# Reordering four engines around the second layer's convolution and cross-attention in a two-layer decoder kernel

## The chip, the cores and the metric

One core of a Trainium2 chip runs the whole program in one launch. The metric is the device time of one execution in microseconds (us), as the median of several executions. PE is the tensor engine, DVE the vector engine, ACT the scalar engine, POOL the GpSimd engine, SP the queue that issues most transfers.

## The reference

Two decoder layers over x, 2 x 1024 tokens of 256 numbers, with a context of 77 rows per batch. Every sublayer is followed by a residual and a layer norm without scale.

```
x = ln(x + L0_attn(x))              # quaternion attention, 16 heads
x = ln(x + L0_xattn(ctx, x))        # two hops of attention to the 77 context rows
x = ln(x + L0_ffn(x))               # 8 experts, 256 tokens each, 256 -> 1024 -> 256, gelu
x = ln(x + L1_attn(x))              # see below
x = ln(x + L1_xattn(x, ctx, ctx))   # 16 heads of 16 numbers, 77 keys
x = ln(x + L1_ffn(x))               # quantised, 256 -> 768 -> 256

def L1_attn(x):                     # a causal convolution with a kernel of powers
    A = sigmoid(A_param)            # K[d, t] = C[d] * A[d]**t * B[d]
    out = conv(x, K) + D * x        # length 1024, per channel
    return layer_norm(x + gelu(out) @ W_proj.T + b_proj) * gamma + beta
```

## The kernel before

It is a kernel without a scheduler: for each engine the instructions are written out by hand in the order in which the engine runs them, and engines wait for each other on counting semaphores. An engine never passes an instruction that waits. X, the 16 tiles of 128 tokens, stays in SBUF. A group is 4 tiles (512 tokens), an expert 2 tiles. PSUM has 8 banks.

**The tail of the first attention.** Sixteen units (a pair of heads of one batch each) run PE, ACT (`exps`) and DVE; after them the second batch's output is turned (`out_turn`, L1721), divided by its denominators on DVE (L1134, L1136), turned again (`att_turn`, L1729), copied by ACT (L638), projected (`out_proj`, L1740), and added to X with a layer norm. A layer norm is always three steps: DVE makes the statistics (L1014, L1017), POOL the power -0.5 (`ln_power`, L388 and L390), DVE subtracts and multiplies (L1022). `ctxR`, the context repeated for each head, is copied by POOL (L466) and is wanted much later, by `context_values`.

**The experts.** For expert e PE runs `hidden(e)` (L1897), ACT the gelu (L701), PE `output(e)` (L1910) into bank 4 or 5, then DVE `expert_stats(e)` (L1281, L1014, L1017) and `expert_norm(e)` (L1022). Before that sum POOL has added the bias b2 to the expert's two tiles of X (L491, one instruction per expert). PE's order is hidden(0), hidden(1), output(0), output(1), hidden(2), hidden(3), and then `x_group_turn` (L1759), which transposes group 0 for the convolution and waits for the norms of experts 0 and 1, output(2), output(3), `projected(0)` and so on. Between the first of these PE makes the keys and values of the second cross-attention (`context_values`, L1885), which DVE masks (L1241, L1243). After the last of them DVE makes the powers of A (L1252) and the convolution's kernels (L1256).

**The convolution** of a group is `convolved(g, k, part)` on DVE (L1269 and L1270, a scan; L1274 and L1275), `conv_gelu` on ACT (L706), `projected(g)` on PE (L1924), then on DVE `conv_out` (L1294), `conv_stats`, `conv_affine(g, 0)` (L1311), `conv_affine(g, 1)` (L1313), `x_stats`, `x_norm`. POOL makes the two operands `XB3[g]` = X + b_proj (L495) and `XG[g]` = X + beta (L498).

**The second cross-attention** starts before the last expert and the last group's convolution are done. It has 32 steps n (a tile and one of two halves of the heads). Each is: `xa_scores(n)` on PE (L1983), `lowest(n)` on DVE (L1351), `numer(n)`, eight exponentials on ACT (L743), `denom(n)` on DVE (L1358, L1359), `weights(n)` on POOL (L524), `p_turn(n)` on PE (L1996) and `p_evac(n)` on ACT (L753, L754). PE's loop at step n issues xa_scores(n + 3) ahead of p_turn(n). Other work is tied to numbers of the loop: `x_turn4` and `queries(1)` to n = 3 and 4 on PE, the four parts of the last group's convolution to n = 0 to 3 on DVE, its gelu to n = 4 on ACT, `projected(3)` to n = 6 on PE. From n = 8 PE also makes the values of the group before (`xa_values`, L2014), the first of which waits for `conv_out(3)`. Everything behind that, to the end of the program, is the same in both kernels.

## Time and profile before

| | us |
|---|---|
| median of 3 runs | 819.36 (818.97 to 822.05) |
| the profiled execution, its time | 822.18 |
| its span, first to last instruction | 820.5 |
| PE busy / DVE / ACT / POOL | 720.7 / 529.3 / 552.2 / 197.8 |

The profiled execution took 1.7 us more than its span, and 2.8 us more than the median of the other runs.

A timeline row gives start, duration, engine, line, operation, tile shapes and count; in brackets stands the idle time just before it and what ended it. A row of the chain of waits gives start, duration and what ran; "issue" is time in which the engine waited for nothing that the profile shows. A row of stretches gives, after the length, the busy time of each engine, then the granted clock of PE (1.00 is 2.4 GHz, 0.50 is 1.2 GHz).

### The profile page before, as it was taken

To read this page: it belongs to the slowest core of one execution; us is meant where nothing else is said; L and a number is where in the kernel's file an instruction comes from. 1 tells how busy PE (TensorE), PEld (TensorE's weight loads), DVE (VectorE), ACT (ScalarE), POOL (GpSimd) and SP (SyncE) were. 2 spreads that over 40 slices of the span, in tenths; PEclk is the share of its full clock that TensorE was granted. 3 is DMA by queue.
4 is the path that set the end of the run, shared out by engine and by line. 5 is a ranking of instruction groups with operands and counts; after the bars stand their busy time and mean duration, and the time that the engine had idled before them with its cause. 6 is when DMAs were issued, how large, how long until landed. Compare 5 with 4: busy or idle time off the path is not lost.

```text
span 820.5 us, 10712 instructions
## 1 busy us (share of the span) xinstructions
PE 720.7 (88%) x3774; PEld 394.6 (48%) x3774; DVE 529.3 (65%) x1215; ACT 552.2 (67%) x971; POOL 197.8 (24%) x232
## 2 busy tenths in 40 slices
PE   4999999899999998999959999678898999992496
PEld 2652222112222227888858887444454744440385
DVE  4694646925223217495458659868976687988886
ACT  3659999999999991653122343586786533798991
POOL 1561142201010003021373113454553200000012
PEclk9899999999999999999989999869998999997698
DMA  7312113122363240230606000002000000000002
GB/s 193 122 26 44 35 26 86 31 66 48 69 193 83 61 121 1 103 103 2 205 0 206 1 1 0 1 0 77 6 34 1 1 0 1 0 1 0 0 26 77
DMA packets 57373, 42.12 MB, mean 51 GB/s; under 512 B 36866, under 2 KB 54120, under 8 KB 57192
## 3 DMA queue, kind: packets, MB, share of 16 engines
q1 hardware_dynamic: 57176, 41.31, 18.1%
q8 instruction: 30, 0.49, 0.3%
q10 hardware_dynamic: 144, 0.13, 0.1%
q14 instruction: 23, 0.19, 0.1%
HBM read 28.59 MB, written 4.46 MB: 40 GB/s over the span
## 4 chain that ended last, share of the span: by engine, by line
PE 60%; ACT 19%; DVE 14%; issue 4%; SPq 1%; DMA 1%; POOL 1%; POOLq 0%; DVEq 0%; ACTq 0%
ACT arena L627 12%; PE banks L1599 8%; PE banks L2139 7%; PE banks L1897 7%; PE banks L1910 6%; PE banks L2147 5%; PE banks L1585 4%; PE banks L1569 3%; PE banks L1759 2%; PE banks L1924 2%; PE banks L1983 2%; DVE arena L1429 2%; PE banks L2027 2%; ACT arena L830 1%; PE banks L1996 1%
## 5 line engine op out<-in xcount | busy, mean ns | idle before, releaser
L627 ACT ACTIVATE arena<-banks 128x1024 f32<-128x1024 f32 x256 | 239.9, 1045 | 8.3 <-PE banks L1599 6.1
L1599 PE MATMUL banks<-arena 128*32 128x512 f32 x1024 | 137.2, 608 | 4.2 <-DVE arena L1091 4.0
L1585 PE MATMUL banks<-arena 64*128 64x512 f16 x512 | 86.6, 385 | 9.0 <-ACT arena L627 5.8
L2139 PE MATMUL banks<-arena 128*128 128x512 f32 x192 | 83.1, 593 | 1.1 <-DVE arena L1445 0.9
L743 ACT ACTIVATE arena<-banks,arena 128x77 f32<-128x77 f32 x256 | 59.3, 366 | 24.5 <-DVE arena L1351 24.5
L388 POOL TENSOR_SCALAR arena<-arena 128x2 f32<-128x2 f32 (+1 forms) x38 | 11.0, 289 | 260.8 <-DVE arena L1017 260.8
L1585 PEld LDWEIGHTS banks<-arena 64*128 64x128 f16 x512 | 20.8, 93 | 108.3 <-ACT arena L627 96.8
L2147 PE MATMUL banks<-arena 128*128 128x256 f32 x192 | 44.4, 396 | 26.8 <-ACT arena L851 26.8
L701 ACT ACTIVATE arena<-banks,arena 128x256 f32<-128x256 f32 x64 | 26.9, 471 | 53.0 <-PE banks L1897 53.0
L1022 DVE TENSOR_SCALAR arena<-arena 128x256 f32<-128x256 f32 x96 | 45.2, 524 | 22.9 <-POOL arena L390 22.9
L2139 PEld LDWEIGHTS banks<-arena 128*128 128x128 f32 x192 | 36.2, 190 | 47.4 <-issue 43.4
L1910 PE MATMUL banks<-arena 128*128 128x256 f32 x256 | 57.0, 382 | 0.0
L1897 PE MATMUL banks<-arena 128*128 128x256 f32 x256 | 56.2, 379 | 0.0
L524 POOL TENSOR_TENSOR arena<-arena 128x616 f32<-128x616 f32 x32 | 40.8, 1275 | 58.7 <-DVE arena L1359 58.7
L2147 PEld LDWEIGHTS banks<-arena 128*128 128x128 f32 x192 | 38.3, 200 | 33.3 <-ACT arena L851 27.6
L1910 PEld LDWEIGHTS banks<-arena 128*128 128x128 f32 x256 | 48.9, 192 | 7.0 <-issue 0.4
L1897 PEld LDWEIGHTS banks<-arena 128*128 128x128 f32 x256 | 48.5, 190 | 6.5
L809 ACT ACTIVATE arena<-banks 128x512 f32<-128x512 f32 x48 | 28.2, 612 | 30.4 <-PE banks L2139 30.4
L1091 DVE COPY arena<-banks 128x512 f32<-128x512 f32 x16 | 10.9, 683 | 53.8 <-PE banks L1599 53.8
L1599 PEld LDWEIGHTS banks<-arena 128*32 128x32 f32 x1024 | 20.5, 108 | 44.9 <-issue 42.7
L1014 DVE BATCH_NORM_STATS2 arena<-arena 128x6 f32<-128x256 f32 x112 | 40.2, 414 | 1.1
L642 ACT ACTIVATE arena<-banks 128x1024 f32<-128x1024 f32 x20 | 20.6, 1028 | 29.1 <-PE banks L1759 28.3
(253 smaller groups left out, 1299.6 us busy)
## 6 DMA issues: line engine op xcount, KB each, us to landing
arena<-in_L_ffn_w SPq DMA_DIRECT2D x16, 1024.0 KB, 7.5
w_kept<-arena SPq DMA_DIRECT2D x3, 768.0 KB, 3.7
arena<-w_kept SPq DMA_DIRECT2D x3, 768.0 KB, 4.7
arena<-in_x SPq DMA_DIRECT2D x4, 512.0 KB, 8.4
out_x<-arena SPq DMA_DIRECT2D x3, 512.0 KB, 2.9
arena<-in_L_ffn_b SPq DMA_DIRECT2D x1, 1024.0 KB, 8.5
arena<-in_L_ffn_w_gate SPq DMA_DIRECT2D x1, 768.0 KB, 7.4
arena<-in_L_ffn_w_up SPq DMA_DIRECT2D x1, 768.0 KB, 9.2
```

The lines of the kernel that those rows point to most:

```text
L524: pool.tensor_tensor(Ex[n % 4], Ex[n % 4], rdx[:, n % 4, :, None].to_broadcast([P, HC, LC]), ALU.mult).then_inc(sem("xa_w"), 1)
L627: act.activation(PT[kt % 2][:, half], PS[:, 2 * (n % 3):2 * (n % 3) + 2, :], ACT.Exp, scale=DH ** -0.5 / QK_UP ** 2).then_inc(sem("exp_don ...
L743: ins = act.activation(Ex[n % 4][:, h, :], PS[:, 2 * (n % 2) + h // 4, LC * (h % 4):LC * (h % 4) + LC], ACT.Exp, scale=-1.0, bias=mxs[:, 8 ...
L809: act.activation((GF if n < IC * G4 else UF)[:, c, 512 * g:512 * g + 512], bank(2 + n % 4), ACT.Copy).then_inc(sem("gu"), 1)
L1014: ins = dve.bn_stats(bstat[:, at + j, :], view(j))
L1022: ins = dve.tensor_scalar(dst(j), src(j), mv[:, at + j, 0:1], rstd[:, at + j:at + j + 1], ALU.subtract, ALU.mult)
L1585: mm = pe.matmul(bank(2 * (n % 3) + h), KT[u % 2][64 * h:64 * h + 64, P * kt:P * kt + P], QT[u % 2][64 * h:64 * h + 64, 512 * half:512 * h ...
L1599: mm = pe.matmul(PS[32 * j:32 * j + 32, 6, :], VS[w][:, kt, h, :], PT[kt % 2][:, half, h, :], start=(kt == 0), stop=(kt == TB - 1))
L1897: mm = pe.matmul(PS[:, f // 2, 256 * (f % 2):256 * (f % 2) + 256], W1r[r][:, k, P * f:P * f + P], XT[:, k, TE * P * e:TE * P * e + TE * P] ...
L1910: mm = pe.matmul(bank(4 + e % 2)[:, D * j:D * j + D], hT[e % 2][:, f, P * j:P * j + P], W2r[r][:, f, :], start=(f == 0), stop=(f == FT - 1))
L2139: mm = pe.matmul(bank(2 + n % 4), (wgT if n < IC * G4 else wuT)[:, k, P * c:P * c + P], XT[:, k, 512 * g:512 * g + 512], start=(k == 0), s ...
L2147: mm = pe.matmul(PS[:, t % 8 // 2, D * (t % 2):D * (t % 2) + D], UF[:, c, P * t:P * t + P], wdT[:, c, :], start=(c == 0), stop=(c == IC - 1))
```

## The change

It edits the order of instructions, and with it some buffers:

1. After the attention units DVE runs `out_norm(3)` behind the divisions of steps 4 and 5 instead of ahead of them. The copy `ctxR` moves from POOL to ACT.
2. POOL adds b2 for experts 0 and 1, once the third set of context values is masked (l1_kv at 4, not 6), and spreads the other six: 2 behind the norm of expert 0, 4 behind that of expert 1. DVE makes the powers ahead of the last two sets of context values, and the norm of expert 0 ahead of the last one; the kernels follow the norm of expert 1.
3. POOL makes X + b_proj and X + beta apart, each earlier. For group 2 they use the buffers of group 0 (`XB3[2]` = `XB3[0]`).
4. PE runs `xa_scores(0)` and `xa_scores(1)` ahead of `projected(2)` (now in banks 5 and 7), then `xa_scores(2)`, the first tile of `output(7)` (now in bank 6), `p_turn(0)`, `xa_scores(3)`, the second tile of `output(7)`, then the loop from n = 1. The turn of group 3, which waits for the last expert's norm, stands behind `p_turn(2)` instead of ahead of the loop. DVE, ACT and POOL are put in a like order; the last convolution's parts stand at n = 2 (two), 3 and 4, its gelu at n = 5.

```diff
@@ pool
-                if q == 3:
-                    pool.wait_ge(sem("mem_ctxT"), 1)
-                    pool.wait_ge(sem("pv_done"), TB * UN)
-                    for b in range(B):
-                        pool.tensor_copy(ctxR[:, b], ...).then_inc(sem("ctx_rep"), 1)
...
-            pool.wait_ge(sem("l1_kv"), 6)
-            for e in range(E):
...
+            pool.wait_ge(sem("l1_kv"), 4)
+            x_plus_b2(0)
+            x_plus_b2(1)
...
             for e in range(E - 2):
                 ln_power(LN_CN[e], 2, 4)
                 g = e // 2
+                pool.wait_ge(sem("ln_c"), e + 1)
+                if e == 0:
+                    x_plus_b2(2)
+                    x_plus_b2(3)
                 if e == 1:
+                    for n in range(4, E):
+                        x_plus_b2(n)
                     pool.wait_ge(sem("l1_wT"), 4)
-                if e in (1, 3):
+                    x_plus_bproj(0)
+                    x_plus_beta(0)
+                if e in (3, 5):
+                    if e == 5:
+                        pool.wait_ge(sem("ln_d2"), 1)
                     x_plus_bproj(g)
-                    x_plus_beta(g)
-                if e in (3, 5):
                     ln_power(LN_DN[2 * g - 2], 4)
                     ln_power(LN_DN[2 * g - 1], 4)
+                    pool.wait_ge(sem("ln_d2"), g)
+                    x_plus_beta(g)
             ln_power(LN_CN[E - 2], 2, 4)
-            x_plus_bproj(2)
-            x_plus_beta(2)
-            ln_power(LN_DN[4], 4)
-            ln_power(LN_CN[E - 1], 2, 4)
+            pool.wait_ge(sem("ln_c"), E - 1)
             x_plus_bo(0)
             weights(0)
             weights(1)
+            ln_power(LN_DN[4], 4)
             for n in range(UX):
                 if n + 2 < UX:
                     weights(n + 2)
+                if n == 0:
+                    ln_power(LN_CN[E - 1], 2, 4)
@@ act
+            act.wait_ge(sem("pv_done"), TB * UN)
+            for b in range(B):
+                act.activation(ctxR[:, b], ..., ACT.Copy).then_inc(sem("ctx_rep"), 1)
...
-            xT_evac(CONV_N[3], 3, 4)
             for n in range(UX):
...
                 p_evac(n)
+                if n == 2:
+                    xT_evac(CONV_N[3], 3, 6)
...
-                if n == 4:
+                if n == 5:
                     conv_gelu(3, 0)
                     conv_gelu(3, 1)
@@ dve
-            out_norm(3)
             for q in range(4, 8 + 3):
...
+                if q == 5:
+                    out_norm(3)
...
+            value_rows(0, 4)
+            value_rows(1, 0)
+            value_rows(2, 1)
+            powers()
+            value_rows(3, 2)
+            expert_stats(0, 4)
+            expert_norm(0, 4)
+            value_rows(4, 3)
+            for e in range(1, E - 2):
                 expert_stats(e, 4)
                 expert_norm(e, 4)
                 g = e // 2
+                if e == 1:
+                    kernels()
...
-            conv_out(2)
-            conv_stats(2)
...
             lowest(0)
+            lowest(1)
+            denom(0)
+            conv_out(2)
+            lowest(2)
+            denom(1)
+            conv_stats(2)
             conv_affine(2, 0)
-            lowest(1)
+            lowest(3)
+            denom(2)
             conv_affine(2, 1)
             expert_stats(E - 1, 4)
-            lowest(2)
+            lowest(4)
             expert_norm(E - 1, 4)
-            denom(0)
-            denom(1)
-            between = {0: lambda: convolved(3, 0, 0), 1: lambda: convolved(3, 0, 1), 2: lambda: convolved(3, 1, 0), 3: lambda: convolved(3, 1, 1),
+            denom(3)
+            between = {2: lambda: (convolved(3, 0, 0), convolved(3, 0, 1)), 3: lambda: convolved(3, 1, 0), 4: lambda: convolved(3, 1, 1),
@@ pe
             output(6)
             queries(0)
-            projected(2)
             xa_scores(0)
             xa_scores(1)
-            output(7)
+            projected(2)
             xa_scores(2)
-            x_group_turn("ln_c", E, CONV_N[3], 3, b0=4)
-            for n in range(UX):
+            output(7, range(0, 1))
+            p_turn(0)
+            xa_scores(3)
+            output(7, range(1, TE))
+            for n in range(1, UX):
...
                 p_turn(n)
+                if n == 2:
+                    pe.wait_ge(sem("proj_y"), 3)
+                    x_group_turn("ln_c", E, CONV_N[3], 3, b0=6)
```

How the rows on an engine move, before first and then changed (line numbers are each kernel's own).

DVE, behind the last attention unit; L1091 is the last unit's copy, L1022 `out_norm(3)`, L1134 and L1136 the divisions of steps 4 and 5:

```order
L1091 COPY arena<-banks 128x512
L1022 TENSOR_SCALAR arena<-arena 128x256 x2
L1134 RECIPROCAL arena<-banks 128x32
L1136 TENSOR_TENSOR arena<-banks,arena 128x256 x2
L1134 RECIPROCAL arena<-banks 128x32
L1136 TENSOR_TENSOR arena<-banks,arena 128x256 x2
```

```order
L1107 COPY arena<-banks 128x512
L1149 RECIPROCAL arena<-banks 128x32
L1151 TENSOR_TENSOR arena<-banks,arena 128x256 x2
L1149 RECIPROCAL arena<-banks 128x32
L1151 TENSOR_TENSOR arena<-banks,arena 128x256 x2
L1038 TENSOR_SCALAR arena<-arena 128x256 x2
```

The norm stands behind both divisions.

POOL, at the start of the experts; L491 (now L487) is the sum with b2, L388 and L390 (now L392 and L394) a norm's power, L495 and L498 (now L496 and L499) the operands of group 0:

```order
L491 TENSOR_TENSOR arena<-arena 128x512 x8
L388 TENSOR_SCALAR arena<-arena 128x2
L390 TENSOR_TENSOR arena<-arena 128x2
L388 TENSOR_SCALAR arena<-arena 128x2
L390 TENSOR_TENSOR arena<-arena 128x2
L495 TENSOR_TENSOR arena<-arena 128x1024
```

```order
L487 TENSOR_TENSOR arena<-arena 128x512 x2
L392 TENSOR_SCALAR arena<-arena 128x2
L394 TENSOR_TENSOR arena<-arena 128x2
L487 TENSOR_TENSOR arena<-arena 128x512 x2
L392 TENSOR_SCALAR arena<-arena 128x2
L394 TENSOR_TENSOR arena<-arena 128x2
L487 TENSOR_TENSOR arena<-arena 128x512 x4
L496 TENSOR_TENSOR arena<-arena 128x1024
```

Two sums instead of eight stand ahead of the first norm's power, two more ahead of the second's, and four behind both.

PE, from `queries(0)` (L1968, now L2012) to the turn of group 3 (L1759, now L1800); L1924 (now L1968) is `projected(2)`, L1983 (now L2027) scores, L1910 (now L1954) `output(7)`, L1996 (now L2041) a `p_turn`:

```order
L1968 MATMUL banks<-arena 128x512 x4
L1924 MATMUL banks<-arena 128x256 x8
L1983 MATMUL banks<-arena 128x308 x4
L1910 MATMUL banks<-arena 128x256 x16
L1983 MATMUL banks<-arena 128x308 x2
L1759 MATMUL banks<-arena 128x128 x8
```

```order
L2012 MATMUL banks<-arena 128x512 x4
L2027 MATMUL banks<-arena 128x308 x4
L1968 MATMUL banks<-arena 128x256 x8
L2027 MATMUL banks<-arena 128x308 x2
L1954 MATMUL banks<-arena 128x256 x8
L2041 MATMUL banks<-arena 128x128 x4
L2041 MATMUL banks<-arena 104x128
L2027 MATMUL banks<-arena 128x308 x2
L1954 MATMUL banks<-arena 128x256 x8
L2027 MATMUL banks<-arena 128x308 x2
...
L1800 MATMUL banks<-arena 128x128 x8
```

Behind the last row but one stand the rest of steps 1 and 2 (three `p_turn` in all and the scores up to n = 5) before the turn of group 3.

## Rows read from the trace of the kernel before

**Rows 1.** The chain of waits, around the first turn for the convolution

```profile
401.72 13.81 PE banks L1897 x64
415.53 8.54 issue
424.08 1.94 PE banks L1759 x8
426.02 14.39 PE banks L1910 x64
```

**Rows 2.** POOL's timeline at the start of the experts

```profile
403.90 14.77 POOL L491 TENSOR_TENSOR arena<-arena 128x512 f32<-128x512 f32 x8 [32.13 <-issue]
...
422.19 0.22 POOL L388 TENSOR_SCALAR arena<-arena 128x2 f32<-128x2 f32 x1 [2.53 <-DVE arena L1017]
```

**Rows 3.** DVE's timeline, same stretch

```profile
385.94 0.49 DVE L1243 TENSOR_TENSOR arena<-arena 128x128 f32<-128x128 f32 x2
...
401.76 0.43 DVE L1241 TENSOR_TENSOR arena<-banks,arena 128x256 f32<-128x256 f32 x1 [6.69 <-PE banks L1885]
...
403.88 5.49 DVE L1252 TENSOR_TENSOR_SCAN arena<-arena 128x1023 f32<-128x1023 f32 x2
...
420.34 0.69 DVE L1281 TENSOR_TENSOR arena<-banks,arena 128x512 f32<-128x512 f32 x1
...
423.24 0.73 DVE L1022 TENSOR_SCALAR arena<-arena 128x256 f32<-128x256 f32 x2 [1.14 <-POOL arena L390]
```

**Rows 4.** PE's timeline behind the first attention's last unit

```profile
310.13 1.97 PE L1721 MATMUL banks<-arena 128*128 128x128 f32 x16 [1.44 <-DVE arena L1091]
```

**Rows 5.** The chain of waits, same stretch

```profile
310.64 2.50 DVE arena L1022 x2
...
314.25 0.99 PE banks L1729 x4
```

**Rows 6.** Stretches: length, busy PE, PEld, DVE, ACT, POOL, then PE's clock

```profile
312.00:314.20 2.20, 0.10 (x1) 0.00 (x0) 2.17 (x5) 0.00 (x0) 0.99 (x1) 1.00 0.00 0
314.20:318.00 3.80, 3.75 (x18) 3.73 (x19) 1.99 (x6) 0.76 (x2) 0.00 (x0) 0.55 0.00 0
```

**Rows 7.** The chain of waits, second cross-attention

```profile
503.12 3.69 PE banks L1924 x16
...
520.96 1.97 PE banks L1759 x8
...
544.38 1.15 ACT arena L706 x2
...
551.39 4.49 PE banks L1924 x16
```

**Rows 8.** Groups by line, 502 to 552 us: total, mean ns of one

```profile
L743 ACT ACTIVATE arena<-banks,arena 128x77 f32<-128x77 f32 x72 | 16.6, 353 | 15.0 <-DVE arena L1351 15.0
L524 POOL TENSOR_TENSOR arena<-arena 128x616 f32<-128x616 f32 x8 | 11.1, 1398 | 14.4 <-DVE arena L1359 14.4
...
L1022 DVE TENSOR_SCALAR arena<-arena 128x256 f32<-128x256 f32 x4 | 7.5, 1926 | 1.6 <-POOL arena L390 1.6
```

**Rows 9.** Groups by line, DVE, 521 to 545 us

```profile
L1358 DVE TENSOR_REDUCE arena<-arena 128x8 f32<-128x616 f32 x7 | 5.4, 776 | 0.0
L1351 DVE TENSOR_REDUCE arena<-banks 128x8 f32<-128x616 f32 x6 | 4.8, 795 | 2.4 <-PE banks L1983 2.3
L1270 DVE TENSOR_TENSOR_SCAN arena<-arena 128x512 f32<-128x512 f32 x2 | 4.2, 2118 | 0.1
L1275 DVE SCALAR_TENSOR_TENSOR arena<-arena 128x512 f32<-128x512 f32 x2 | 3.2, 1586 | 0.1
L1269 DVE TENSOR_TENSOR arena<-arena 128x512 f32<-128x512 f32 x2 | 1.8, 924 | 0.0
...
L1274 DVE TENSOR_TENSOR arena<-arena 128x512 f32<-128x512 f32 x2 | 1.3, 641 | 0.0
```

**Rows 10.** PE's timeline at the first xa_values

```profile
559.63 1.94 PE L2014 MATMUL banks<-arena 128*64 128x512 f32 x8 [0.65 <-DVE arena L1294]
```

More of the change, by code:

```diff
@@ L241, in decoder @@
         early = at(20480, 24576)
-        XB3 = [m(4, D) for m in (early, early, late, late)]
-        XG = [m(4, D) for m in (early, early, late, late)]
+        XB3 = [m(4, D) for m in (early, early, late)]
+        XG = [m(4, D) for m in (early, early, late)]
+        XB3.insert(2, XB3[0])
+        XG.insert(2, XG[0])
         e0 = at(0, 8192)
@@ L1235, in _, with value_rows @@
             dve.sem_inc(sem("l1_kv"), 1)
-            for n, i in enumerate((4, 0, 1, 2, 3)):
+            def value_rows(n, i):
                 rows = ROWS[i]
@@ L1322, in x_norm @@
                 return normalise(view, view, 4)
-            for e in range(E - 2):
+            value_rows(0, 4)
[7 more added lines that the diff above has]
+            for e in range(1, E - 2):
                 expert_stats(e, 4)
@@ L1406, in _ @@
                        28: lambda: residual(2, 0), 29: lambda: residual(2, 1), 30: lambda: xa_stats(2), 31: lambda: xa_norm(2)}
-            for n in range(UX):
+            for n in range(2, UX):
                 if n + AHEAD < UX:
```

86 lines of the change are left out of this document (51 added, 35 removed).

## The prediction

> **What bounds the kernel now.** The table gives PE 720.7 us busy of 820.5, but that is an average over stages; I read where PE stands still on the chain of waits, and then, on the timelines of the other engines, what it stands for. Three places matter here.
>
> At 415.53 PE stops for 8.54 us between two dense stretches of matmuls, and the turn behind the gap takes 1.94 us [rows 1], where 16 such transposes, twice as many, take 1.97 [rows 4]: half the clock. The view calls the gap "issue"; the code says that the turn waits for the norms of experts 0 and 1, and DVE ends the second of them at 423.97 [rows 3]. That norm is late since POOL adds b2 for all eight experts in one go, 14.77 us from 403.90 to 418.67, and only then makes the powers of the two norms, the second at 422.19 [rows 2].
>
> Behind the last attention unit PE turns step 4 from 310.13 and its next piece starts at 314.25 [rows 4, 5]. DVE spends 2.50 us of that on `out_norm(3)` [rows 5], two instructions that take 0.73 elsewhere [rows 3]; the copy of ctxR runs on POOL at that time. PE's clock from 314.2 to 318 is 0.55 [rows 6].
>
> In the cross-attention's first steps no engine is full. The chain goes from the second norm (POOL sums beside it: L1022 takes 7.5 us for four instructions that need 1.5 when alone) [rows 8, 3] to the turn of group 3 at 520.96, through the last convolution to `projected(3)` at 551.39 [rows 7] and to the first `xa_values` at 559.63 [rows 10]. From there on both kernels are the same, so what counts is when that point is reached.
>
> **The change, part by part.**
>
> *A, the attention's tail.* The divisions of step 4 need only the first 8 of the 16 transposes that start at 310.13 and take 1.97 [rows 4], so they start at 311.1 and not at 313.14, when the norm ends [rows 5]; ends at 312.3, and PE goes on at 312.35 instead of 314.25: 1.9 us. The norm itself slides into a wait of DVE behind step 5. PE's wait shrinks from 2.15 to about 0.3; the wait of 1.44 ahead of it [rows 4] did not lower the clock, which stayed at 1.00 until 314.2 [rows 6], so I expect full clock where it was 0.55 for 3.8 us, of which 1.7 could go [rows 6]; I take 1.4, since the divisions pace PE too. A = 3.3. If the clock falls all the same it is 1.9, and at most 3.6. The copy of ctxR costs ACT two instructions of 1232 elements; nothing here shows one. Two gelus of 512 take 1.15 [rows 7], so at their price both together take 2.8, and I bound them by 2 and 5. ACT is free from the end of the last unit at 308.7 [rows 4] until its first copy at 313.3: 4.6 us of cover. At 5 us, 0.4 of A would go.
>
> *B, the experts' start.* The third set of context values is masked at 386.4 [rows 3]; POOL then adds b2 for two experts, 2 x 1.85 us [rows 2], done at 390.1. DVE: powers 5.5 [rows 3] (386.6 to 392.1), the fourth set 2.0 from 393.1 (PE sets that time, as before: 40 matmuls at 13.81 / 64 [rows 1], 8.6 us, ahead of the last set at 401.76), expert 0's sum and statistics 1.8 (420.34 to 422.10 for expert 1 [rows 3]) to 396.9, POOL's power 1.1, norm 0.7 [rows 3]: done at 398.7. POOL adds two more, to 402.4. The last set runs from 401.76 to 403.7 as before [rows 3]; sum and statistics to 405.5, power and norm to 407.4. PE asks at 415.53 [rows 1]: 8 us of slack, so the gap goes whole, 8.54. The turn returns to full clock, 1.94 to 0.97, and the 64 matmuls behind it to the 13.81 of the same shape, from 14.39 [rows 1]: 0.97 + 0.58. B = 10.1, from 8.5 if the clock has another cause. The cover to look at next is the convolution of group 0: DVE starts it 1 us behind the turn, at 417.5, and POOL still runs (four sums, then X + b_proj and X + beta, to about 419.4). Its four parts take 10.5 at the prices of the last group's [rows 9] and the gelu 0.6 [rows 7], so it ends at 428.6 at the latest that a row shows, and PE asks for it at 415.53 + 0.97 + 13.81 = 430.3. If POOL held DVE longer than that, each us would cost one.
>
> Queued transfers: expert e's weights are asked for by SP when output(e - 4) is done; that moves with PE, so the distance stays.
>
> *C, the cross-attention's start*, on the clock of before (A and B left out). PE has queries done and ACT's copy at 503.1 [rows 7]. Then two scores (about 2 at most), projected(2) 3.7, scores 1, the first tile of output(7) 3.45 (16 matmuls of rows 1's shape), which brings p_turn(0) to 512.3 to 513.3. Its weights are ready before: lowest(0) 0.8 at 504.7, numer(0) 1.84 (16.6 / 9) at 506.6, denom 1.0 at 507.6, weights 1.4 at 509 [rows 8, 9]. So the wait that is new in the middle of output(7) costs nothing, with 3 to 4 us to spare; behind it queue the scores, the second tile and with it expert 7's norm. The second tile ends at 517.2 to 518.8.
>
> DVE up to expert 7's norm: it now has two more `lowest` (1.6) and three `denom` (3.0) ahead of that norm [rows 9], and loses the collision of two norms with POOL's sums, 7.5 to 1.5, 6.0 [rows 8, 3]. Its waits grow by about 2.5 (numer(0), and projected(2), which ends 1 us later). The turn of group 3 then starts at 520.96 [rows 7] - 6.0 + 1.6 + 3.0 + 2.5 = 522, 1 later than before. But steps 0 to 2 are behind PE by then, where before they all stood ahead.
>
> From the turn to projected(3), DVE bound: four denom 4.0, three lowest 2.4, the four parts of the convolution 10.5 [rows 9], so 16.9 from 522: 538.9; the two gelus 1.15 [rows 7] and a table load of about as much: 541.3, where it was 551.39 [rows 7]. From there to the first xa_values 8.2 as before [rows 7, 10]: 549.5 against 559.63. That is 10.1; I take off 1 for some ten hops between engines not priced here. C = 9. For the upper bound, every instruction of the parts at the price of the fastest, 0.64 [rows 9], saves 5.4 more, of which POOL's and ACT's own work leave perhaps 4: 13. For the lower, the 28.5 us from the end of the turn to projected(3) [rows 7] lose only DVE's own work of the three steps that are gone, 3 x 1.8 [rows 9]: 523 + 23.1 = 546.1, C = 5.
>
> Of the parts' 10.5, two scans take 2.12 each [rows 9], though the powers' scans are twice as long and took 2.7 each, beside POOL's sums too [rows 3]. The Trainium skill (GPSIMD Engine Reference, Key points) says that GpSimd shares its SBUF interfaces with VectorE and contends with instructions that have two SBUF inputs. By that rule the parts meet POOL's weights and X + b_proj again, and C stays at 9; without it C would be near 13. The rows on L1022 agree with it (7.5 against 1.5). The same rule speaks against the new place of the powers beside POOL's sums, but the 5.49 was measured there already.
>
> **The sum.** 3.3 + 10.1 + 9 = 22.4. The profiled execution's 822.18 becomes 799.8; it stood 2.8 above the median of 819.36, which becomes 797.0. I predict 797.
>
> **Rivals.** *R1: the cross-attention gives nothing back.* p_turn(0) and the scores hold up output(7), or DVE's new list runs 9 us longer than I count, so that group 3's turn slips and values start at 559 again. For it: the turn has no slack, and DVE's list behind it is full. Against: the two collisions vanish. C of 0 to 3: about 804.5. *R2: the 8.54 us stay in part*, if what held the norm was not POOL's eight sums, or if DVE's new list is late. Rows 2 and 3 speak against it: the power follows the sums by nothing. B of 2: 805. *R3: both*, 811 to 815. *R4: more than the sum*, if the parts of the convolution run alone and the clock stays up in 520 to 550: 789 to 791. *R5, slower: the clock.* PE falls to 1.2 GHz behind short waits (2.15 us at 312 [rows 4 to 6]), and the new order leaves short ones between steps. What is won is lost where 22.4 us of dense matmuls run at half the clock, and 27 make the kernel slower by over 0.5%, 824. Against it: the stretch behind the longest wait, 8.54 us, lost 0.97 + 0.58 and was then at full clock [rows 1]. The Trainium skill (TensorE: Matmul & The Clock Gate, What's actually happening) says that the ratio follows how busy the PE has been, which is in favour of the changed kernel, as its waits are shorter.
>
> **Chances.** The sum as it stands (18 to 27 us won) 0.62; R1 0.14; R2 0.07; R3 0.05; R4 0.08; R5 0.04. The range 791 to 806 holds the first, most of R1 and R2 and part of R4, 0.81. A measurement of this kernel can tell about 0.5% (4 us) from no change. Faster by more than that: 0.94 (all but R5 and a little of R3); within it 0.03; slower 0.03.
>
> **What the profile would show.** A: L1134's counterpart starts near 311, PE's gap ahead of the next turn is under 0.5, the clock at 1.00. B: no gap ahead of the first turn for the convolution, POOL in sums of 2, 2 and 4. C: the wait ahead of p_turn(0) under 0.3; the turn of group 3 some 12.4 us earlier than 520.96 (A and B, less 1); projected(3) near 529 and the first xa_values near 537 in the new trace. Behind that, a constant shift of about 22. Wrong would be: a gap of some us in the middle of output(7), a gap ahead of projected(0), or a stretch behind xa_values that has lost clock.

## The result

| | before | after |
|---|---|---|
| median of 4 runs, us | 819.16 (816.18 to 822.05) | 795.79 (794.31 to 796.66) |
| ratio of the medians | | 0.9711, 95% interval 0.9687 to 0.9735 |
| the profiled execution, its time / span | 822.18 / 820.5 | 796.66 / 794.9 |
| PE busy / DVE / ACT / POOL | 720.7 / 529.3 / 552.2 / 197.8 | 710.1 / 519.3 / 554.1 / 196.9 |

The changed kernel is 23.4 us faster by the medians and 25.5 by the two profiled executions. The forecast was 797 us.

PE's timeline after, from the last unit of the attention to the first turn of the memory stage:

```profile
306.73 1.07 PE L1640 MATMUL banks<-arena 128*32 128x512 f32 x8
309.23 1.97 PE L1762 MATMUL banks<-arena 128*128 128x128 f32 x16 [1.43 <-DVE arena L1107]
311.57 0.66 PE L1770 MATMUL banks<-arena 128*128 128x128 f32 x4 [0.37 <-DVE arena L1151]
...
322.10 1.04 PE L1800 MATMUL banks<-arena 128*128 128x128 f32 x8
```

The gap ahead of the next turn, 2.15 us before (it ended at the row 314.25 in [rows 5]), is 0.37. From the start of the unit's last eight matmuls (306.73; before 307.63) to the turn at 322.10 (before 326.44) it is 15.37 us, where it was 18.81: 3.44 won. DVE and ACT in the same stretch:

```profile
310.36 0.36 DVE L1149 RECIPROCAL arena<-banks 128x32 f32<-128x32 f32 x1 [1.19 <-PE banks L1762]
...
312.48 0.73 DVE L1038 TENSOR_SCALAR arena<-arena 128x256 f32<-128x256 f32 x2
```

```profile
307.93 2.36 ACT L648 ACTIVATE arena<-arena 128x1232 f32<-128x1232 f32 x2 [1.63 <-PE banks L1640]
```

The divisions start at 310.36, before the norm, and the norm at 312.48 takes 0.73, not 2.50 [rows 5]. The stretches that answer to [rows 6]:

```profile
311.10:313.30 2.20, 1.83 (x17) 1.74 (x17) 2.17 (x8) 0.60 (x1) 0.00 (x0) 1.00 0.00 0
313.30:317.10 3.80, 3.80 (x27) 3.47 (x25) 2.68 (x9) 1.09 (x2) 0.00 (x0) 1.00 0.01 4
```

The clock is 1.00 in both; it was 0.55 in the second.

The chain of waits after, around the first turn for the convolution:

```profile
397.29 13.81 PE banks L1938 x64
411.10 0.87 PE banks L1800 x8
411.97 13.81 PE banks L1954 x64
425.79 3.45 PE banks L1968 x16
```

Against [rows 1] the line "issue" of 8.54 us is gone, and the turn takes 0.87 instead of 1.94. In the timelines hidden(2) starts at 397.12 and hidden(4) at 429.08, 31.96 us apart; before these were 401.56 and 443.70, 42.14 apart: 10.2 won. POOL's timeline, then DVE's two norms:

```profile
382.19 6.54 POOL L487 TENSOR_TENSOR arena<-arena 128x512 f32<-128x512 f32 x2 [14.78 <-issue]
...
403.20 5.90 POOL L487 TENSOR_TENSOR arena<-arena 128x512 f32<-128x512 f32 x4 [0.85 <-DVE arena L1038]
```

```profile
393.83 0.73 DVE L1038 TENSOR_SCALAR arena<-arena 128x256 f32<-128x256 f32 x2 [1.15 <-POOL arena L394]
...
402.39 0.73 DVE L1038 TENSOR_SCALAR arena<-arena 128x256 f32<-128x256 f32 x2 [1.14 <-POOL arena L394]
```

The norm of expert 1 is done at 403.1, 8.0 us ahead of PE's turn. Two of POOL's sums took 6.54, not the 3.7 that I had from [rows 2].

PE's timeline in the cross-attention's start:

```profile
497.56 0.71 PE L2041 MATMUL banks<-arena 128*128 128x128 f32 x5
...
507.78 1.06 PE L1800 MATMUL banks<-arena 128*128 128x128 f32 x8 [2.04 <-issue]
...
520.90 0.79 PE L2027 MATMUL banks<-arena 64*128 64x308 f32 x4 [2.78 <-ACT arena L750]
...
523.58 1.40 PE L2027 MATMUL banks<-arena 64*128 64x308 f32 x4 [1.19 <-ACT arena L758]
...
526.69 5.49 PE L1968 MATMUL banks<-arena 128*128 128x256 f32 x16 [0.46 <-ACT arena L721]
...
535.93 1.51 PE L2059 MATMUL banks<-arena 128*64 128x512 f32 x6 [0.65 <-DVE arena L1317]
```

There is no wait at p_turn(0) (497.56). The turn of group 3 is at 507.78, projected(3) at 526.69, the first `xa_values` at 535.93. From hidden(4) that is 106.85 us, where it was 115.93 (443.70 to 559.63 [rows 10]): 9.1 won. The waits that remain are for expert 7's norm (2.04 us ahead of the turn at 507.78; the view calls it "issue"), for POOL's weights and for ACT. DVE's norm of expert 6 and the parts of the last convolution:

```profile
487.83 0.73 DVE L1038 TENSOR_SCALAR arena<-arena 128x256 f32<-128x256 f32 x2 [1.15 <-POOL arena L394]
...
510.15 2.63 DVE L1290 TENSOR_TENSOR arena<-arena 128x512 f32<-128x512 f32 x1
512.82 2.12 DVE L1291 TENSOR_TENSOR_SCAN arena<-arena 128x512 f32<-128x512 f32 x1
...
518.01 0.65 DVE L1290 TENSOR_TENSOR arena<-arena 128x512 f32<-128x512 f32 x1
```

The norm fell from 4.79 us to 0.73; in the convolution, 2.63 and 2.12 us stand beside POOL's X + b_proj and weights, against 0.65 for the same form as the first at 518.01.

### The profile page after: what moved, and what is told of

Read it like the earlier page. It is cut to its first block, busy times and chain, and to the rows that moved or that the text cites. A ratio compares the mean times of both kernels' runs of the same rounds, so it can differ in the third digit from the quotient of the medians.

```text
span 794.9 us, 10723 instructions
## 1 busy us (share of the span) xinstructions
PE 710.1 (89%) x3774; PEld 386.9 (49%) x3774; DVE 519.3 (65%) x1216; ACT 554.1 (70%) x973; POOL 196.9 (25%) x230
## 4 chain that ended last, share of the span: by engine, by line
PE 56%; ACT 22%; DVE 16%; issue 3%; DMA 1%; SPq 1%; POOL 1%; POOLq 0%; DVEq 0%; ACTq 0%
ACT arena L638 12%; PE banks L1640 8%; PE banks L2189 7%; PE banks L1938 7%; PE banks L1954 6%; PE banks L1626 4%; PE banks L1610 3%; PE banks L1968 2%; DVE arena L1470 2%; DVE arena L1030 2%; PE banks L1800 2%; PE banks L2072 2%; PE banks L2027 1%; ACT arena L846 1%; ACT arena L857 1%
## 5 line engine op out<-in xcount | busy, mean ns | idle before, releaser
L638 ACT ACTIVATE arena<-banks 128x1024 f32<-128x1024 f32 x256 | 239.8, 1045 | 8.5 <-PE banks L1640 6.1
L392 POOL TENSOR_SCALAR arena<-arena 128x2 f32<-128x2 f32 (+1 forms) x38 | 11.9, 313 | 250.2 <-DVE arena L1033 250.2
L1954 PE MATMUL banks<-arena 128*128 128x256 f32 x256 | 56.6, 380 | 0.0
L1954 PEld LDWEIGHTS banks<-arena 128*128 128x128 f32 x256 | 48.2, 190 | 7.2 <-issue 0.8
L1038 DVE TENSOR_SCALAR arena<-arena 128x256 f32<-128x256 f32 x96 | 37.3, 442 | 18.3 <-POOL arena L394 18.3
L1107 DVE COPY arena<-banks 128x512 f32<-128x512 f32 x16 | 10.9, 683 | 54.2 <-PE banks L1640 54.2
L394 POOL TENSOR_TENSOR arena<-arena 128x2 f32<-128x2 f32 (+1 forms) x38 | 36.5, 960 | 3.2
```

The lines of the kernel that those rows point to most:

```text
L394: pool.tensor_tensor(rstd[:, at:at + n], veps[:, at:at + n], expo[:, at:at + n], ALU.pow).then_inc(sem("ln_rstd"), 1)
L638: act.activation(PT[kt % 2][:, half], PS[:, 2 * (n % 3):2 * (n % 3) + 2, :], ACT.Exp, scale=DH ** -0.5 / QK_UP ** 2).then_inc(sem("exp_don ...
L1038: ins = dve.tensor_scalar(dst(j), src(j), mv[:, at + j, 0:1], rstd[:, at + j:at + j + 1], ALU.subtract, ALU.mult)
L1954: mm = pe.matmul(bank(Y_BANK[e])[:, D * j:D * j + D], hT[e % 2][:, f, P * j:P * j + P], W2r[r][:, f, :], start=(f == 0), stop=(f == FT - 1))
```

## The experiments

Each kernel was timed beside the kernel before, whose own median was 817.5 to 819.2 in these sets, so kernels of different sets are compared by their ratios. The times of one kernel lie up to 5.6 us to either side of its median, so the readings are taken stage by stage from PE's timelines: A is from the last unit's eight matmuls to the first turn of the memory stage, B from hidden(2) to hidden(4), C from hidden(4) to the first `xa_values`, and the tail from there to PE's last matmul.

| run | A | B | C | tail | median us | ratio to before, 95% |
|---|---|---|---|---|---|---|
| before | 18.81 | 42.14 | 115.93 | 254.5 | 819.16 | |
| e1 (A alone) | 15.35 | 43.47 | 114.49 | 253.9 | 817.14 | 0.9987 (0.9964 to 1.0010) |
| e2 (norm moved, copy on POOL) | 15.36 | 43.01 | 116.43 | 254.8 | 817.73 | 0.9988 (0.9963 to 1.0012) |
| e3 (B alone) | 18.81 | 31.96 | 116.31 | 254.8 | 809.33 | 0.9880 (0.9859 to 0.9901) |
| e6 (wait for 4 alone) | 17.14 | 33.88 | 114.63 | 254.5 | 808.66 | 0.9876 (0.9851 to 0.9901) |
| e5 (B, sums at once) | 17.15 | 31.95 | 116.23 | 255.0 | 807.97 | 0.9887 (0.9860 to 0.9914) |
| e4 (A and B) | 15.36 | 31.95 | 114.79 | 254.7 | 806.91 | 0.9860 (0.9837 to 0.9883) |
| e9 (A, B, sums early) | 15.36 | 31.96 | 116.32 | 254.8 | 804.61 | 0.9841 (0.9809 to 0.9872) |
| e10 (changed, sums late) | 15.37 | 31.95 | 109.26 | 254.7 | 798.90 | 0.9765 (0.9747 to 0.9783) |
| e7 (changed, projection first) | 15.36 | 31.96 | 110.69 | 252.8 | 798.90 | 0.9770 (0.9750 to 0.9790) |
| e8 (changed, output whole) | 15.37 | 31.95 | 108.18 | 254.6 | 799.25 | 0.9768 (0.9743 to 0.9793) |
| e12 (scores alone between halves) | 15.36 | 31.95 | 106.78 | 252.5 | 794.92 | 0.9730 (0.9706 to 0.9754) |
| e11 (b_proj before weights) | 15.36 | 31.96 | 104.47 | 253.8 | 796.15 | 0.9722 (0.9690 to 0.9753) |
| after | 15.37 | 31.96 | 106.85 | 252.5 | 795.79 | 0.9711 (0.9687 to 0.9735) |

**Part A: which of its two moves counts.** e1 is the kernel before with the norm moved and the copy on ACT; e2 moves only the norm:

```diff
-            out_norm(3)
             for q in range(4, 8 + 3):
...
+                if q == 5:
+                    out_norm(3)
                 if 6 <= q < 8 + 2:
```

and e1 takes the copy along:

```diff
-                        pool.tensor_copy(ctxR[:, b], ctxT[:, :, None, LC * b:LC * b + LC].to_broadcast([P, KD, HC, LC]))
...
+                act.activation(ctxR[:, b], ctxT[:, :, None, LC * b:LC * b + LC].to_broadcast([P, KD, HC, LC]), ACT.Copy)
```

> The kernel before with part A alone: out_norm(3) behind the divisions of step 5, and the copy of ctxR on ACT instead of POOL. My theory (A is worth what it was priced at, by itself): 3.3 to 3.5 us less than the kernel before; PE's wait of 2.15 us ahead of L1729's counterpart becomes about 0.4, the clock behind it stays at 1.00 and the first turn of the memory stage comes 3.4 us earlier than 326.44, counted from the last unit's matmuls. The 8.54 us of PE ahead of the first turn for the convolution stay as they are. Rival (the trace after began 0.9 us early for another reason, and part of what I put down to A is such drift): 2.4 us or less. Rival 2 (what A wins is given back at a later wait): under 1 us in the time, with the turn early all the same.

> The kernel before with only out_norm(3) moved behind the divisions of step 5; the copy of ctxR stays on POOL, where it runs at 310.6 to 313.0 in the trace before. It asks whether the 2.50 us of the norm (0.73 elsewhere) are the norm's or the copy's. Theory 1 (the copy slows any instruction of DVE beside it): the divisions now stand beside the copy and take up to 1.8 us longer, PE's wait stays near 2, and the kernel wins 0 to 1 us. Theory 2 (it slows only instructions that read and write the large memory, and the divisions read the matmul banks): the divisions keep their 1.1 us a pair, PE's wait falls to about 0.4 and the kernel wins the same 3.3 us as with the copy on ACT.

Both took 15.4 us in A. So the moved norm is all of it, and putting the copy on ACT adds nothing to it in this stage. POOL's copy and DVE's work in e2:

```profile
307.90 2.37 POOL L466 COPY arena<-arena 128x1232 f32<-128x1232 f32 x2
```

```profile
309.00 0.75 DVE L1135 TENSOR_TENSOR arena<-banks,arena 128x256 f32<-128x256 f32 x2
...
310.73 0.73 DVE L1022 TENSOR_SCALAR arena<-arena 128x256 f32<-128x256 f32 x2
```

The copy (307.90 to 310.27) stands beside a division at 309.00 that takes its usual 0.75, and the norm, which now starts when the copy has ended, takes 0.73. Theory 2 holds for the divisions. In the times e1 stands 2.0 us lower by its median and 1.1 by its ratio, e2 1.0 by its ratio, and neither is clear of no change: less than the 3.3 expected. The stage A of e1 has the whole 3.46, but in B, which it does not alter, the turn and the matmuls behind the same 8.55 us gap took 1.3 longer, at a granted clock of 0.84 where the kernel before has 0.91. So part of what A wins is missing later, as in rival 2, but by the clock and not by a later wait. In e2 stage B took 0.9 longer in the same way; whether that is chance or follows from A, these traces cannot tell. Neither interval reaches 0.996, what 3.4 us would be: in the times A is worth less than in these two traces.

**Part B: which of its moves counts.** e3 is the kernel before with B alone. e6 changes one number of the kernel before:

```diff
             pool.wait_ge(sem("ffn_b_in"), 16)
-            pool.wait_ge(sem("l1_kv"), 6)
+            pool.wait_ge(sem("l1_kv"), 4)
             for e in range(E):
```

> The kernel before with part B alone: POOL adds b2 in sums of 2, 2 and 4 from the third masked set on, with the powers of the norms between, and DVE's powers, expert 0 and the last sets in the changed order; the rest of POOL's list (X + b_proj, X + beta) stays as before. My theory (B is worth 10.1 by itself, and the wait is the whole of it): 10 us less, no gap of PE ahead of the first turn for the convolution, the turn at full clock (0.87 to 1.0 us). Rival (the gap goes but its work is late at the next asker, since here both X + b_proj and X + beta still follow the last four sums): a gap of some us ahead of projected(0) or of hidden(4), and 4 to 8 us less. Rival 2 (the tail drift of about 1.9 us seen behind the first xa_values belongs to B): 12 us less.

> The kernel before with one number changed: POOL's eight sums of b2 wait for 4 instead of 6 steps of l1_kv, so they start at the third masked set (386.4) and run in one go; DVE's order is that of before. If only the sums held the norm of expert 1 (the reading of rows 2 and 3), what is left is DVE's own order: sum and statistics of expert 0 at 412.7 behind the powers and CBrev, norm 0 at 416.3, norm 1 done at 420.0 instead of 423.97: the gap shrinks from 8.54 to about 4.5 and the kernel wins 4 us, up to 5.5 if the scans at 403.88, without POOL beside them, are shorter than 5.49. Rival 1 (the sums were not what held it): nothing. Rival 2 (the sums alone were all of it): 8.5 to 10 us.

POOL, DVE and PE of e6:

```profile
386.16 9.95 POOL L491 TENSOR_TENSOR arena<-arena 128x512 f32<-128x512 f32 x8 [14.76 <-issue]
```

```profile
403.41 4.50 DVE L1252 TENSOR_TENSOR_SCAN arena<-arena 128x1023 f32<-128x1023 f32 x2
...
407.95 1.53 DVE L1256 TENSOR_SCALAR arena<-arena 128x1024 f32<-128x1024 f32 x2
...
415.97 0.74 DVE L1022 TENSOR_SCALAR arena<-arena 128x256 f32<-128x256 f32 x2 [1.14 <-POOL arena L390]
```

```profile
416.81 1.07 PE L1759 MATMUL banks<-arena 128*128 128x128 f32 x8 [1.74 <-issue]
```

e3 won the 10.2 in stage B, and 9.9 by its median (10 expected). For e6 I had expected 4 to 5.5 us; stage B fell by 8.3. The eight sums took 9.95 us with DVE mostly idle (14.77 beside its scans [rows 2]), and in return DVE's two scans took 4.50 (5.49 [rows 3]) and the two instructions that make the convolution's kernels (CBrev) 1.53 (3.25 at 409.41 before). Moving POOL away shortened DVE's own list by 2.7 us on top of the 4, and the turn and the matmuls behind it took 1.5 less, at full clock. What stays is a wait of 1.74. In the time e6 and e3 cannot be told apart; the stage tells them apart by 1.9 us.

e5 is e3 with the eight sums in one go:

```diff
-            def x_plus_b2(e):
+            pool.wait_ge(sem("ffn_b_in"), 16)
+            pool.wait_ge(sem("l1_kv"), 4)
+            for e in range(E):
...
-            x_plus_b2(0)
-            x_plus_b2(1)
...
-                    x_plus_b2(2)
-                    x_plus_b2(3)
...
-                    for n in range(4, E):
-                        x_plus_b2(n)
```

> The kernel before with part B, but POOL's eight sums of b2 in one go from the third masked set on, ahead of the power of norm 0 (not 2, 2 and 4 with the powers between). DVE's order is the changed one. The run with the wait for 4 alone had its eight sums done in 9.95 us, and the one with part B its first two, beside the scans, in 6.54; so here about 6.5 + 6 x 1.24 = 14 us from 381.5 to 395.5, norm 0 at 397.2 where it was done at 393.9, norm 1 at about 402.5 and PE asks at 410.3. Theory (the split itself buys nothing, all of B comes from the earlier start and from the scans no longer standing between the last sets and the norms): no gap of PE, and 32.0 us from hidden(2) to hidden(4) as with part B. Rival (the power has to go between the sums): a gap of 1 us or more.

```profile
382.07 14.08 POOL L491 TENSOR_TENSOR arena<-arena 128x512 f32<-128x512 f32 x8 [14.87 <-issue]
```

```profile
389.11 2.14 DVE L1244 TENSOR_TENSOR arena<-arena 104x128 f32<-104x128 f32 x2
...
397.18 0.73 DVE L1022 TENSOR_SCALAR arena<-arena 128x256 f32<-128x256 f32 x2 [1.39 <-POOL arena L390]
```

Stage B took 31.95, as with the split. The sums took 14.08 (14 expected) and norm 0 came at 397.18. An instruction pair of a masked set, 0.49 before, took 2.14 beside them, and nobody waited for it. So of the 10.2 us the earlier start of the sums gives 8.3, DVE's order, added to it, the other 1.9, and the split into 2, 2 and 4 nothing. DVE's order alone, with the late sums, was not run.

**Part C against its cover.** e4 is the kernel before with A and B; what it lacks to the changed kernel is C.

> The kernel before with parts A and B together, without C (the changed kernel less its new start of the cross-attention). From hidden(4) to the first xa_values it should take what the kernel before takes, 115.9 us, where the changed kernel takes 106.9; up to hidden(4) it should stand where the changed kernel does. So in the time 13.6 us less than the kernel before, 9 to 10 more than the changed kernel. Rival (C works only through A and B, or they through it): a stretch behind hidden(4) that differs from 115.9 by over 2 us.

Its stage C took 114.79, within the 2 us of 115.9 that were allowed, and the eight traces with the old order in it 114.5 to 116.4, mean 115.6. The changed kernel and e12 have 106.85 and 106.78: C is worth 8.8 to 9.1. By the times it is more, 11.1 by the medians (806.91 less 795.79) and 12 by the ratios; the tails of the two traces differ by 2.2. Against the kernel before, e4 won 11.4 by the medians where 13.6 were expected and stand in its stages A and B: as in e1, the time shows less than they do.

**C: the collision of expert 6's norm with POOL's sums.** e9 adds to e4 only the sums' new place; e10 takes it back in the changed kernel:

```diff
                 if e in (3, 5):
-                    if e == 5:
-                        pool.wait_ge(sem("ln_d2"), 1)
-                    x_plus_bproj(g)
+                    if e == 3:
+                        x_plus_bproj(g)
...
             ln_power(LN_CN[E - 2], 2, 4)
+            x_plus_bproj(2)
+            x_plus_beta(2)
```

> Parts A and B and, of C, only POOL's X + b_proj and X + beta of group 2 ahead of expert 6's norm (and the buffer that goes with it); the order of PE, DVE and ACT in the cross-attention is that of before. The norm of expert 6 then takes 0.73 us where it took 4.79. Theory (that saving falls into the wait for output(7), which ends at 515.1 in the trace before and which DVE takes up at 515.24): under 1 us of the 115.9 from hidden(4) to the first xa_values. Rival (the collision is worth its 4 us by itself, as my sum has it): 112.

> The changed kernel with POOL's X + b_proj and X + beta of group 2 back behind the power of expert 6's norm, where the kernel before has them; PE, DVE and ACT as changed. Then the norm of expert 6 (two TENSOR_SCALAR, 0.73 us now) runs beside them again and should take about 4.8 us as it did before, and POOL's weights(0) come 4.7 us later, 1.2 more than their spare time. If that collision is the part of C that I put at 6.0 us: 3 to 5 us more than the changed kernel from hidden(4) to the first xa_values (106.9). Rival (the lost DVE time lies in a wait for PE's output(7)): under 1 us.

DVE in e9, then in e10:

```profile
486.21 0.74 DVE L1035 TENSOR_SCALAR arena<-arena 128x256 f32<-128x256 f32 x2 [1.15 <-POOL arena L392]
490.59 1.22 DVE L1312 TENSOR_TENSOR arena<-banks,arena 128x1024 f32<-128x1024 f32 x1 [3.65 <-PE banks L1952]
...
501.90 2.75 DVE L1035 TENSOR_SCALAR arena<-arena 128x256 f32<-128x256 f32 x2 [0.47 <-POOL arena L392]
```

```profile
486.22 4.79 DVE L1040 TENSOR_SCALAR arena<-arena 128x256 f32<-128x256 f32 x2 [1.52 <-POOL arena L394]
...
508.08 0.73 DVE L1040 TENSOR_SCALAR arena<-arena 128x256 f32<-128x256 f32 x2 [0.47 <-POOL arena L394]
```

In e9 the norm takes 0.74 and DVE then stands 3.65 us for projected(2); the turn of group 3 comes 77.25 us behind hidden(4), where it is 77.26 in the kernel before. The saving of 4 us is worth nothing in the old order. In the new order the same collision costs 3.1 at the turn (81.81 against 78.70) and at projected(3), and 2.4 at `xa_values`, since projected(3) took 4.79 in e10 and 5.49 in the changed kernel. I had expected 3 to 5 at `xa_values`.

**C: the order on PE.** e7 puts projected(2) back ahead of the first scores; e8 makes output(7) one piece; e12 keeps the halves with only the scores between. In this order:

```diff
             queries(0)
+            projected(2)
             xa_scores(0)
             xa_scores(1)
-            projected(2)
```

```diff
-            output(7, range(0, 1))
+            output(7)
             p_turn(0)
             xa_scores(3)
-            output(7, range(1, TE))
```

```diff
             output(7, range(0, 1))
-            p_turn(0)
             xa_scores(3)
             output(7, range(1, TE))
+            p_turn(0)
```

> The changed kernel with projected(2) ahead of the first two score groups again; all else as changed. If the order of the scores is what C lives on: DVE's list begins with lowest(0), which then comes 3.65 us later, and with it numer, denom and weights(0) (3.4 us to spare ahead of p_turn(0)) and, behind DVE's list, norm 7 and the turn of group 3: 1.5 to 3.6 us more than the changed kernel from hidden(4) to the first xa_values (106.9). Rival (DVE waits elsewhere in that list for as long, so the order of scores and projection is worth nothing): within 0.5 us of 106.9.

> The changed kernel with output(7) in one piece, and p_turn(0) and the scores of step 3 behind it. p_turn(0) then comes 3.5 us later and the expert's output ends 1.4 us earlier. My theory (the two halves carry little, since steps 1 and 2 wait for ACT and DVE and not for this turn): within 1 us of the changed kernel from hidden(4) to the first xa_values. Rival (the early turn is what puts steps 0 to 2 behind PE before group 3's turn): 2 to 4 us more.

> The changed kernel with only the scores of step 3 between the two halves of output(7), and p_turn(0) behind the second half. With output(7) in one piece DVE waited 2.84 us in lowest(3) for those scores and group 3's turn came 2.8 us later. Theory (what the halves are worth is the earlier scores, p_turn(0) between them is worth nothing): the turn of group 3 at 78.7 us behind hidden(4) as in the changed kernel, projected(3) at 97.6, the first xa_values at 106.9, each within 0.5. Rival (the P turn between matters, since ACT's copies of it stand ahead of the exponentials of step 3): ACT's numer(3) and with it lowest and denom of step 3 come later, and the turn of group 3 or projected(3) by 1 us or more.

DVE at `lowest(3)` in e8, and PE in e8 at projected(3):

```profile
498.49 0.80 DVE L1386 TENSOR_REDUCE arena<-banks 128x8 f32<-128x616 f32 x1 [2.84 <-PE banks L2027]
```

```profile
525.42 3.72 PE L1968 MATMUL banks<-arena 128*128 128x256 f32 x16 [1.15 <-ACT arena L721]
```

In e7 DVE waits 4.38 us for its first scores (0.67 in the changed kernel), the turn comes 3.4 later and `xa_values` 3.8 (1.5 to 3.6 expected). In e8 DVE waits 2.84 for the scores of step 3 behind the whole of output(7); turn and projected(3) come 2.8 later, but projected(3) then runs at full clock (3.72 us; 5.49 in the changed kernel), so at `xa_values` 1.3 are left. My theory had "within 1 us" and was wrong on the mechanism: the halves matter. e12 shows why: with the scores alone between them every mark (78.71, 97.61, 106.78) is the changed kernel's. The P turn between the halves is worth nothing; the scores between them are worth 2.8 at the turn.

These runs explain why the turn of group 3 is hardly later than before. The larger gain stands in the stretch behind it, from the turn to projected(3): 30.2 us before, and 18.9 to 19.1 in the changed kernel and in e7, e8, e10 and e12 alike. C's 9.1 are these 11.3, less 1.4 at the turn and 0.8 behind projected(3). The rows show what went, PE before, then DVE and ACT after:

```profile
548.73 1.40 PE L1983 MATMUL banks<-arena 64*128 64x308 f32 x4 [4.12 <-ACT arena L743]
```

```profile
523.18 1.59 DVE L1296 SCALAR_TENSOR_TENSOR arena<-arena 128x512 f32<-128x512 f32 x1
525.49 1.15 ACT L721 ACTIVATE arena<-arena 128x512 f32<-128x512 f32 x2
```

DVE ended the convolution's last part 20.6 us behind the turn before (at 541.58) and 17.0 after (524.77), with six `denom` and four `lowest` in it before and four and three after. ACT ended the gelu 3.95 us behind that before (its row 544.38 in [rows 7]), having copied `queries(1)` first, and 1.87 after. And projected(3) started 5.65 us behind the gelu before, since PE first waited until 548.73 for ACT's exponentials of another step, and 0.05 after. That is 3.6, 2.1 and 5.6 of the 11.3. PE has seven `p_turn` between turn and projected(3) before and four after. No run takes the turn's new place, or the gelu's, back alone, so this share of C is read from the two traces and not tested.

**A version to beat both.** e11 puts POOL's X + b_proj of group 3 ahead of weights(3):

```diff
                 if n == 0:
                     ln_power(LN_CN[E - 1], 2, 4)
-                if n == 1:
                     x_plus_bproj(3)
```

> The changed kernel with POOL's X + b_proj of group 3 ahead of weights(3) instead of behind it, so that it runs from 507.6 to 510.0 on the clock of the changed kernel, beside DVE's reductions, and not from 509.9 to 512.2 beside the first part of the last convolution (whose 128x512 TENSOR_TENSOR took 2.63 there, 0.65 in the second part). It is the one edit by which the experiments might beat the changed kernel. Theory (the collision is on the path to projected(3)): that TENSOR_TENSOR falls to 0.7 to 1.3 us, projected(3) comes 1 to 2 us earlier than 97.6 behind hidden(4), the first xa_values up to as much. Rival 1 (the collision only changes its partner: weights(3) and (4), 1.2 us later, now stand beside the same instruction and the scan): within 0.5. Rival 2 (weights(3) is late for p_turn(3)): PE's wait there grows from 0.4 to 1.6, and nothing comes of it.

```profile
512.55 1.69 DVE L1289 TENSOR_TENSOR arena<-arena 128x512 f32<-128x512 f32 x1
```

```profile
528.15 3.72 PE L1967 MATMUL banks<-arena 128*128 128x256 f32 x16 [1.63 <-ACT arena L720]
```

The convolution's first instruction took 1.69 instead of 2.63 (0.7 to 1.3 expected); only weights stand beside it now. projected(3) came 0.94 earlier (96.67), a little under the 1 to 2 expected. `xa_values` came 2.4 earlier; the rest of that goes with the clock at projected(3). The tail took 1.3 longer, so its time cannot be told from that of e12 on the same chip (796.15 against 794.92).

## Why the prediction was right

**A, 3.3 predicted, 3.44 measured.** The wait fell from 2.15 to 0.37 (about 0.3 said) and the clock stayed up. The clock's share is seen apart: e5 and e6, with the order of before and its wait of 2.15, took 17.15 and 17.14 in A, not 18.81, and in the 3.8 us behind the wait their clock is 1.00, where it is 0.55 before [rows 6] and 0.61 in e3. So the wait alone is 1.8, and 1.7 is the clock, which an execution may lose there or not. Over the four traces with the old order (18.81 twice, 17.14, 17.15; mean 17.98) A is worth 2.6, still more than e1's ratio shows (1.1, with an interval that ends just under 3); the 3.3 was right for the profiled execution and high for the median. The copy on ACT took 2.36 (2.8 estimated) and is done at 310.3, before ACT is wanted.

**B, 10.1 predicted, 10.2 measured** (10.9 against the mean of the three traces that have the gap whole, 42.87). The steps: norm 1 done 8 us ahead of PE, as said; the turn at 0.87 and the matmuls at 13.81, as said. Two errors did no harm. POOL's first two sums took 6.54 beside the scans, priced at 3.7, and nobody waited for them. The convolution of group 0 was done 4.4 us ahead of PE's call for it (421.39 against 425.79), where I had left 1.7, having priced its parts at the last group's contended rows. And the split, which I counted as part of B, is not needed, as e5 shows.

**C, 9 predicted, 8.8 to 9.1 measured.** I had DVE as the bound up to the turn of group 3: less 6.0 for the collisions, plus 7.1 for the new work and waits, so 1 us later. Measured: 1.44 later (78.70 against 77.26), and DVE's list has these terms. The norm of expert 6 starts 58.8 us behind hidden(4) in both traces and takes 4.1 less; the two `lowest`, three `denom` and waits up to expert 7's sum add 7.5; that expert's norm takes 2.0 less. The list is the bound in the new order: PE ends output(7) at 502.6, and DVE takes it up at 504.04 (before, at 515.24, as soon as PE had ended it). e10 agrees, since giving the 4.1 back moves the turn by 3.1. That the same 4 us were worth nothing in the old order (e9), where DVE would have stood for PE's projected(2), I had not seen; taken from the place of the old turn, as I took them, they were no saving, and the sum held because the new list fills them with work. Of the 7.5, 0.9 are a collision that I had not counted. POOL's weights of step 2 (501.57 to 502.93) stand beside a part of `conv_affine(2, 1)`, which took 1.66 before and 2.59 after, in DVE's list just ahead of expert 7's sum:

```profile
501.41 2.59 DVE L1341 SCALAR_TENSOR_TENSOR arena<-arena 128x256 f32<-128x256 f32 x4
```

The next stretch held: turn to projected(3) 18.9 us (19.3 predicted, 30.2 before), with DVE's list up to the last part's end at 17.0 (16.9 priced) and 1.9 for the table load and the gelus (2.4 priced). The last one, 8.2 predicted, took 9.24 (8.45 before in the timeline), since projected(3) ran partly at half clock, 5.49 us where the timeline before has 4.70 and full clock gives 3.72. PE started projected(3) 0.05 behind the gelus, where it was 5.65 before; I had taken that for granted and said no reason. The terms miss by 0.4 more at the turn, 0.4 less up to projected(3) and 1.0 more behind it, and the 1 us that I took off for hops between engines covers just that: as it names nothing that the trace shows, the closeness of C is in part luck.

**The shift behind `xa_values`** was not constant: 23.7 us there and 25.6 in the spans. The 1.9 go with the clock:

```profile
629.63:639.63 10.00, 10.00 (x43) 6.93 (x44) 4.01 (x9) 5.37 (x23) 2.76 (x3) 0.72 0.00 0
769.76:779.76 10.00, 9.99 (x34) 8.38 (x35) 7.04 (x11) 10.00 (x13) 0.00 (x0) 0.73 0.00 0
```

```profile
605.93:615.93 10.00, 10.00 (x53) 7.51 (x53) 5.28 (x13) 6.62 (x25) 3.65 (x3) 0.86 0.00 1
744.83:754.83 10.00, 10.00 (x37) 8.52 (x38) 7.04 (x11) 10.00 (x13) 0.00 (x0) 0.80 0.00 0
```

These are the same two stretches of the program, of before and of after; the clock is 0.72 and 0.73 in the one, 0.86 and 0.80 in the other. Another 0.9 us was won ahead of stage A, where the kernels do not differ. So the sum of 22.4 stands against 22.7 (3.44 + 10.2 + 9.1) in the parts, and the profiled execution's 25.5 hold 2.8 that none of the three parts explains.

**The rivals.** R1, R2 and R3 did not occur. R4's condition, parts that run free of POOL, did not either: the scans took 2.12 again, as the row at 512.82 shows, where the same form in group 0's convolution, with no POOL instruction beside it, took 1.22:

```profile
414.30 1.22 DVE L1291 TENSOR_TENSOR_SCAN arena<-arena 128x512 f32<-128x512 f32 x1
```

e11 shows what one such collision is worth, 0.94. The Trainium skill (GPSIMD Engine Reference, Key points) says that GpSimd shares its SBUF interfaces with VectorE and contends with instructions of it in a 2-port mode or with two SBUF inputs; e6 agrees that they slow each other, 9.95 against 14.77 us for POOL and 1.53 against 3.25 for DVE. The prediction named only two inputs and took the rows on L1022 for agreement; L1022 has one tensor input, so these rows do not bear on that half of the rule, and DVE's scans and its TENSOR_TENSOR of 128x512, which have two, do. R5, the clock, is real in small: projected(3) took 1.8 us more than at full clock, 0.8 more than before.

What stays open: in after, e7 and e12 the tail took 252.5 to 252.8 and projected(3) 5.4 to 5.8 us; in the other eleven traces the tail took 253.8 to 255.0. Whether the longer projected(3) and the shorter tail have one cause was not tried.

## What to carry to other kernels

When a list of one engine grows by an instruction, look first at what the wait for the next engine hides: a saving of 4 us ahead of an instruction that waits for PE was worth nothing in the old order and 2.4 us in the new one. Before splitting a block of work, try starting it earlier: one changed wait gave 8.3 of 10.2 us, partly because DVE and POOL, no longer side by side, both got faster. When several parts win a few us each, read them as stages in the trace, from mark to mark, since the whole time scatters by more than a part is worth.

## What the hardware showed beyond what I had expected

Between these traces the same instructions differ mostly by the granted clock; where the clock is the same a stage repeats to a few hundredths (A 15.35 to 15.37, B 31.95 to 31.96). The stretch from 20 to 40 us, the same in all kernels, in e7 and in e11:

```profile
20.00:40.00 20.00, 19.48 (x85) 12.88 (x86) 15.47 (x22) 13.71 (x32) 14.56 (x22) 1.00 0.36 121
```

```profile
20.00:40.00 20.00, 18.28 (x66) 11.49 (x67) 12.88 (x18) 12.53 (x28) 11.57 (x17) 0.83 0.34 119
```

The clock is 1.00 and 0.83 there; over the first 100 us it is 1.00 and 0.95, over the next 100 us 1.00 and 0.98. The attention's last eight matmuls start at 302.47 in e7 and at 309.05 in e11: 6.6 us apart, in instructions in which the two kernels do not differ. Behind the same gap of 8.5 us stage B took 42.14, 43.01 or 43.47. The Trainium skill (TensorE: Matmul & The Clock Gate, What's actually happening) says that the ratio follows how busy the PE has been; the mean clock of the span agrees, 0.950 before and 0.969 after in the profiled executions, with the waits gone. The same section says that the point at which the clock comes up varies between executions of one kernel; the two rows agree, and no run here shows more of the why.

POOL beside DVE slows both, but not for every form. The eight sums took 1.24 us each with DVE mostly idle and 1.85 on average when they began with the scans; two that lay wholly beside the scans took 3.27 each. A DVE pair of 104x128 took 0.49 or 2.14; the division that reads the matmul banks took 0.75 either way, and in e11 a `denom` beside POOL's X + b_proj kept its 0.79.
